# Spreading a kernel's side work one piece per hidden block, and grouping four square roots

## The reference

```python
q = jnp.einsum('btd,sd->bts', x, Wq) + bq      # k and v alike
def step(S, qkv_t):
    S = d[None, :, None] * S + v_t[:, :, None] * k_t[:, None, :]
    return (S, jnp.einsum('bij,bj->bi', S, q_t))
attn = x + jnp.einsum('bts,ds->btd', scan_out, Wo) + bo
x = _layernorm(x + attn)
gate = jnp.einsum('bsd,hd->bsh', x, wg);  up = jnp.einsum('bsd,hd->bsh', x, wu)
x = _layernorm(x + jnp.einsum('bsh,dh->bsd', jax.nn.silu(gate) * up, wd))
```

## Time and profile before

| | us |
|---|---|
| the two timed runs | 2865.55 and 2637.14, median 2751.35 |
| the profiled execution | 2553.9 |
| its span, slowest core (of 2532.6 to 2552.1) | 2552.1 |
| TensorE busy in it | 2290.6 |
| VectorE busy | 538.3 |
| ScalarE busy | 382.6 |
| GpSimd busy | 255.2 |

### The profile page before, as it was taken

One profiled execution on the slowest core, in us unless ns is written; L12 is line 12 of the kernel. 1 busy time (PEld: TensorE's weight loads), 2 busy tenths in 40 slices (PEclk: granted clock), 3 DMA queues, 4 the chain that ended last, 5 costly groups with the idle time before them and its releaser, 6 DMA issues.

```text
span 2552.1 us, 30492 instructions; the slowest of 8 cores (2532.6 to 2552.1 us)
## 1 busy us (share of the span) xinstructions
PE 2290.6 (90%) x11224; PEld 1088.7 (43%) x11429; DVE 538.3 (21%) x1082; ACT 382.6 (15%) x595; POOL 255.2 (10%) x244
## 2 busy tenths in 40 slices
PE   2653899989999899998999899998999989999996
PEld 1331345444454344443454444543454434434443
DVE  2400203221032202132032221222030320221002
ACT  1100212012110212012120121102120121101100
POOL 0000110011100111011100111001100111001100
PEclk9686999999999999999999999999999999999998
DMA  6895122312133122222223121331213212132212
GB/s 137 122 118 107 60 82 70 104 67 67 59 97 111 50 83 76 74 99 67 75 75 108 59 75 54 100 104 58 75 46 95 83 58 74 47 127 67 91 44 81
DMA packets 62390, 206.79 MB, mean 81 GB/s; under 512 B 7123, under 2 KB 7123, under 8 KB 60644
## 3 DMA queue, kind: packets, MB, share of 16 engines
q1 hardware_dynamic: 55748, 152.07, 19.1%
q0 software_dynamic: 6496, 52.76, 9.5%
HBM read 206.90 MB, written 35.65 MB: 95 GB/s over the span
## 4 chain that ended last, share of the span: by engine, by line
PE 83%; DMA 8%; DVE 3%; another core or an unknown queue 2%; issue 2%; ACT 1%; DVEq 0%; POOL 0%; ACTq 0%; SPq 0%; POOLq 0%
PE pb L617 26%; PE pb L633 25%; PE pb L723 24%; DMA wg_s<-wgT 2%; PE pb L301 2%; DMA wu_s<-wuT 2%; PE pb L464 2%; DMA wd<-wd_s 2%; PE pb L536 1%; DVE htmp L650 1%; PE pb L334 1%; DMA xA<-x 1%; PE pb L268 1%; DVE aoTl L442 1%
## 5 line engine op out<-in xcount | busy, mean ns | idle before, releaser
L617 PE MATMUL pb<-x1Tl,wg 128*128 128x512 bf16 x1536 | 592.8, 386 | 7.1 <-issue 2.7
L633 PE MATMUL pb<-x1Tl,wu 128*128 128x512 bf16 x1536 | 582.5, 379 | 3.0
L723 PE MATMUL pb<-wd,hTl 128*128 128x512 bf16 x1528 | 579.3, 379 | 3.7
L617 PE MATMUL pb<-x1Th,wg 128*128 128x512 bf16 x1458 | 564.2, 387 | 5.5 <-ACT sg L643 5.5
L723 PE MATMUL pb<-wd,hTh 128*128 128x512 bf16 x1458 | 553.0, 379 | 17.3 <-DVE htmp L650 9.6
L633 PE MATMUL pb<-x1Th,wu 128*128 128x512 bf16 x1479 | 561.1, 379 | 0.0
L650 DVE SCALAR_TENSOR_TENSOR htmp<-pb,sg 128x512 f32<-128x512 f32 x192 | 132.8, 692 | 1158.1 <-PE pb L633 1059.3
L665 POOL TENSOR_TENSOR hTl<-htmp,hTh 128x512 bf16<-128x512 f32 x192 | 228.9, 1192 | 1213.3 <-ACT hTh L658 1188.6
L617 PEld LDWEIGHTS pb<-x1Th,wg 128*128 128x128 bf16 x1536 | 152.4, 99 | 197.7 <-issue 24.7
L723 PEld LDWEIGHTS pb<-wd,hTh 128*128 128x128 bf16 x1528 | 148.9, 97 | 201.5 <-issue 30.8
L658 ACT CAST hTh<-htmp 128x512 bf16<-128x512 f32 x192 | 118.6, 617 | 761.8 <-DVE htmp L650 761.8
(11 more groups left out here) (127 smaller groups left out, 1153.1 us busy)
## 6 DMA issues: line engine op xcount, KB each, us to landing
wg<-wg_s SPq DMA_DIRECT2D x96, 512.0 KB, 3.4
wu<-wu_s SPq DMA_DIRECT2D x96, 512.0 KB, 3.2
wd<-wd_s SPq DMA_DIRECT2D x192, 256.0 KB, 2.6
out<-x POOLq DMA_DIRECT2D x30, 512.0 KB, 2.9
xA<-x POOLq DMA_DIRECT2D x4, 2048.0 KB, 7.6
xB<-x POOLq DMA_DIRECT2D x4, 2048.0 KB, 8.3
wd_s<-wdT POOLq DMA_DIRECT2D x1, 6144.0 KB, 55.6
wg_s<-wgT POOLq DMA_DIRECT2D x1, 4608.0 KB, 48.6
```

What stands on the lines that cost most here:

```text
L617: lambda e, off=off, dc=dc, xsrc=xsrc, rot=rot, xi=xi: e.matmul(PS[rot][:, 0:512], wg[:, off:off + 128], xsrc[:, dc * CHUNK:(dc + 1) * CHUNK],
L633: lambda e, off=off, dc=dc, xsrc=xsrc, rot=rot, xi=xi: e.matmul(PS[rot][:, 512:1024], wu[:, off:off + 128], xsrc[:, dc * CHUNK:(dc + 1) * ...
L723: lambda e, hc=hc, s=s, par=par, hsrc=hsrc, xi=xi, pbase=pbase: e.matmul(PS[pbase + s // 2][:, (s % 2) * 512:(s % 2 + 1) * 512], hsrc[:, h ...
```

## The change

It has two parts. In the gate/up loop one thunk is taken behind each block, where it was two behind each of the first twelve. And `t_ln1` of sub-chunks 0 to 2 now ends with the scaled variance; that of sub-chunk 3 issues all four square roots, and then the four pairs of reciprocal and normalisation. The number of instructions is the same in both kernels, except for the loads of ScalarE's function tables, which are put in where the function changes.

```diff
-                o_std = p.add("scalar", ... AF.Sqrt, deps=[o_ve], tag="std1_%d_%d" % (n, s))
-                o_rs = p.add("vector", ... reciprocal ..., deps=[o_std], tag="rs1_%d_%d" % (n, s))
-                o_ap = p.add("vector", ... tensor_scalar(x1p(n, s), ...), deps=[o_rs], tag="ap1_%d_%d" % (n, s))
-                st[("ap", s)] = o_ap
+                st[("ve", s)] = o_ve
+                if s < NSUB - 1:
+                    return
+                stds = []
+                for s2 in range(NSUB):
+                    sb = SB1(s2)
+                    stds.append(p.add("scalar",
+                                      lambda e, sb=sb: e.activation(
+                                          stats[:, sb + 5:sb + 6], stats[:, sb + 4:sb + 5],
+                                          AF.Sqrt),
+                                      deps=[st[("ve", s2)]], tag="std1_%d_%d" % (n, s2)))
+                for s2 in range(NSUB):
+                    sb = SB1(s2)
+                    o_rs = p.add("vector", ... reciprocal ..., deps=[stds[s2]], tag="rs1_%d_%d" % (n, s2))
+                    o_ap = p.add("vector", ... tensor_scalar(x1p(n, s2), ...), deps=[o_rs], tag="ap1_%d_%d" % (n, s2))
+                    st[("ap", s2)] = o_ap
@@ the gate/up loop of ffn
-                pump(2 if hc < 12 else 1)
+                pump(1)
```

More of the change, by code:

```diff
@@ new lines, in t_ln1 @@
+                stds = []
[8 more added lines that the diff above has]
+                    sb = SB1(s2)
+                    o_rs = p.add("vector",
+                                 lambda e, sb=sb: e.reciprocal(
+                                     stats[:, sb + 6:sb + 7], stats[:, sb + 5:sb + 6]),
+                                 deps=[stds[s2]], tag="rs1_%d_%d" % (n, s2))
+                    o_ap = p.add("vector",
+                                 lambda e, s2=s2, sb=sb: e.tensor_scalar(
+                                     x1p(n, s2), x1p(n, s2),
+                                     stats[:, sb + 2:sb + 3],
+                                     stats[:, sb + 6:sb + 7],
+                                     ALU.add, ALU.mult),
+                                 deps=[o_rs], tag="ap1_%d_%d" % (n, s2))
+                    st[("ap", s2)] = o_ap
```

## The result

The changed kernel takes 2490.62 us (median of 10 runs, lowest 2487.86), the kernel before, run beside it, 2554.09 (median of 8, lowest 2552.54). The ratio is 0.9751, 95% interval 0.9739 to 0.9763: faster by 2.5%. The two timed runs shown ahead of the prediction (2637 and 2866 us), one more of before and two of the changed kernel were executions in which cores of one or both dies had a lower clock, and no ratio here uses such executions. The profiled execution's slowest core has a span of 2488.2 us, against 2552.1.

What follows compares the result with a forecast made beforehand. TensorE, busy 2290.6 of 2552.1 us, was taken as the bound. Per chunk 10.3 + 0.6 - 0.5 - 1.2 = 9.2 us, times 7 = 64, so 2553.9 - 64 = 2490 us; range 2470 to 2700.

Steps and rivals of the forecast that it cites:

- `t_proj`: A block between `t_ao` and `t_proj` cuts TensorE's wait for `aoTl` to 0.65 us; gain 10.3 us a chunk.
- The clock: After 7.6 us without a matmul at `t_proj` TensorE runs at 1.2 GHz; gate matmuls behind take 5.43 us, elsewhere 3.45.
- Scans and seams: Gate/up loop: scans behind single blocks gain 0.6 us a chunk; three more seams at 0.16 us lose 0.5.
- The group: Four square roots together delay normalisation in down half 0: 1.2 us lost a chunk, at most 4.8; second transposes just in time.
- The table loads: 28 fewer on ScalarE, 36 us (74 us by the skill page), counted as nothing because TensorE doesn't wait there.
- The head: Chunk start: 24.3 us of TensorE work against silu of block 0 ending at 19.5 us; 4.8 us cover, nothing lost.
- The rival: Chunk head uncovered, TensorE waits 5.5 us for silu with no slow matmuls, seven times: 2528 us; chance 0.06.
- Chunk 0: The 68.9 us wait at `t_kt` moves to up of block 3; counted as nothing, within 1 us.
- The period of a chunk: Time from one chunk's head to the next falls by 9 us.
- the likeliest case: Whole kernel: the forecast of 2490 us, own range 2473 to 2502 (7.4 to 11.5 us a chunk); chance 0.68.
- its two faster outcomes: Over 2% faster: the forecast, chance 0.68, and ScalarE's loads on the path, 2454 us, chance 0.05; together given as 0.72.
- The slower rival: Denser matmuls on eight cores lower TensorE's clock; 5% lower gives 2605 us; chance 0.06.

Runs made afterwards that it cites:

- The one seam by itself: Kernel before with a block put between `t_ao` and the first `t_proj`, nothing else moved apart: 2483.67 us, ratio 0.9719.
- the filler matmuls: Kernel before plus 28 matmuls that nobody reads between `t_ao` and the first `t_proj` of chunks 1 to 7: 2534.42 us, ratio 0.9917.
- the two kernels that separate it: Changed kernel with the layer norm of before: 2482.56 us; changed kernel with the pump of before, keeping the grouped square roots: 2564.16 us.
- the head laid open: Changed kernel with no side work behind the first two blocks of a chunk: 2544.63 us, ratio to before 0.9978.
- part 1 alone: One thunk behind each block as in the changed kernel, but the layer norm as before: 2482.56 us, ratio 0.9715 to before.

## Why the prediction was right, step by step

- *The bound and the place.* TensorE sets the time, and the gain was where the chain of waits put it. The one seam by itself gives 72 us; the changed kernel gives 63.5, as its second edit costs 8.
- *`t_proj`.* Forecast: 10.3 us a chunk, with 0.65 us of wait left. Measured from the one-seam kernel: 72 / 7 = 10.3, and a wait of 2.9 / 7 = 0.4. The earlier trace rows carried this: the chain inside `t_ao` took 7 us at either place.
- *The clock.* Right, and shown apart by the filler matmuls: 21 of the gain's 72 us.
- *Scans and seams.* Forecast +0.6 and -0.5; each seam costs 0.11 us instead of 0.16 (the 16 gate matmuls behind a piece take 3.56 us, elsewhere 3.45). The balance over 7 chunks is 1.1 us by the difference of two kernels: as good as nothing, as forecast.
- *The group.* Forecast 1.2 us a chunk from a sum over VectorE's rows; the trace has 8.9 / 7 = 1.3, the two kernels that separate it 8.1 and 8.4 us in all. The second transposes came just in time in chunks 0 to 5. In chunk 6 they did not: the sum was read from chunk 1, where `t_xt` and a block of down matmuls lie between two `t_x1`. There TensorE waited 3.4 us more for `x1Tl`. Before waited there too (3.8 us), but without the 1.3 us for the normalisation and at the full clock; now 8 matmuls take 1.66 us too long on the slowest core. So one thing that the prediction said would not be seen was: a stage behind 240 us, other than the last chunk's head, with a clock under 0.95.
- *The table loads.* Worth nothing, as TensorE's waits said, though 35 us of ScalarE's time went. What a load is worth depends on who waits: with the head laid open, one stood on the chain. The Trainium skill ("ScalarE: Activation LUTs", "Rules for kernel authors") advises to do all functions of one table set before switching, and that did save 28 loads. Its 1283 ns for the load ("What ACT_TABLE_LOAD costs") is the trace's. The drain that it adds, for 2.66 us in all, is not in the trace: before, the last square root ahead of chunk 2's first silu ends at 809.85 and the silu starts at 811.23, 1.38 us later with the load between them. So the 74 us of the prediction were 35.3 by measurement.

```profile
809.65 0.20 ACT L777 ACTIVATE stats<-stats 128x1 f32<-128x1 f32 x1 [3.93 <-DVE stats L772]
809.93 1.28 ACT L643 ACT_TABLE_LOAD   x1
```

- *The head.* Forecast: 4.8 us of cover left and no wait. None came. The rival's price was put at 5.5 us times 7 without slow matmuls; the kernel that opens the head has six heads, 5.6 us each and 1.9 us or more of slow matmuls behind. The rival was undersized: at least 45 us and not 39.
- *Chunk 0.* Forecast: the wait moves to the up matmuls of block 3, for nothing. It did; it is 66.7 us against 68.9, and 69.0 with part 1 alone.
- *The period of a chunk.* Forecast: 9 us less. In the two chains the heads of chunks 2 and 3 are 296.97 us apart before (792.30 to 1089.27) and 286.93 in the changed kernel (771.78 to 1058.71), 10.0 less; between the heads of chunks 1 and 2 it is 8.6 less. Single chunks miss the forecast by about 1 us either way, so that the whole sum is right within 1 us, 64 against 63.5, is in part luck.
- *The range.* The time lies in the likeliest case's own range, 2473 to 2502; for its lower bound of 7.4 us a chunk the prediction gives no working, and the chances of its two faster outcomes add up to 0.73 and not 0.72. The wide upper end was set by the two timed runs of before, and was not needed.
- *The slower rival.* The stages of down half 1 keep 1.00 in the profiled execution, so the denser matmuls didn't lower the clock in it.

## What to carry to other kernels

When side work is woven into a loop of matmuls, look for the two neighbouring pieces of which the second needs what another engine makes of the first, and put at least that chain's length of matmuls between them; how evenly the rest is spread hardly matters. Price the gap with the slow matmuls behind it, which a wait of 7.6 us brought here and one of 0.7 us didn't (waits of 1.3, 2.5 and 0.9 us close together did on the slowest core). Before a group of operations is formed to save an engine's time, see whether anyone waits for that engine, and who waits for the operations that the group delays.

## What the runs showed of the hardware

A load of 512 KB that lands in 3.4 us by the median of the kernel before took 48.7 us beside one large conversion, with the DMA engines 0.99 busy. Cut into paced pieces of 512 KB, the conversion left the loads at 5.5 and 6.3 us (medians). And a VectorE subtraction of 0.28 us took 0.95 us in `t_ao` where GpSimd's subtraction ran beside it, and 0.28 when that was held back.
